# Lookup steps of 512 columns and whole grams in a DLRM interaction tower

## What is computed

```python
e = jnp.stack([tbl_0[ids[:, 0]], ..., tbl_25[ids[:, 25]]], axis=1)     # 2048 x 26 x 128
combined = jnp.concatenate([e, r_dense_x[:, None, :]], axis=1)
interact = jnp.einsum('bfd,bgd->bfg', combined, combined)
z = interact[:, _TRIU_I, _TRIU_J]                                      # 351 pairs
h = jnp.concatenate([z, r_dense_x], axis=1)
h = jnp.maximum(h @ W_top1 + b_top1, 0.0)                              # 479 -> 512
h = jnp.maximum(h @ W_top2 + b_top2, 0.0)                              # 512 -> 256
y = h @ W_top3                                                         # 256 -> 1
```

## Time and profile before

| | us |
|---|---|
| median of 3 executions | 373.93 (371.11 to 374.2) |
| the profiled execution | 374.13 |
| its span in the profile | 371.9 |
| TensorE busy | 345.5 |
| GpSimd busy | 258.8 |

### The profile page before, as it was taken

The page is one execution under the profiler, slowest core; times in us unless marked ns, Lnnn a source line. Parts: engine busy times, 40 slices in busy tenths (PEclk is TensorE's granted clock), DMA queues, the critical chain, the costliest instruction groups (busy, mean ns, idle before and its releaser), DMA issues.

```text
span 371.9 us, 13580 instructions
## 1 busy us (share of the span) xinstructions
PE 345.5 (93%) x6176; PEld 317.1 (85%) x6176; DVE 170.1 (46%) x380; ACT 184.4 (50%) x235; POOL 258.8 (70%) x265
## 2 busy tenths in 40 slices
PE   1998787989998999999999999999999999999997
PEld 0898776879897889999899998999899998899887
DVE  4589654533533435356245535356244635350220
ACT  3588242764345543473716643473725734376433
POOL 6688877777777777777777777777777777774000
PEclk9999899999998999999999999999999999999999
DMA  7967743211622126221262226321262222221000
GB/s 242 356 183 243 232 149 107 67 51 51 196 70 67 51 58 183 78 65 51 68 198 53 65 54 173 91 67 53 51 206 60 64 53 65 55 56 37 19 4 3
DMA packets 15917, 37.14 MB, mean 100 GB/s; under 512 B 5141, under 2 KB 7829, under 8 KB 15860
## 3 DMA queue, kind: packets, MB, share of 16 engines
q0 software_dynamic: 8192, 16.79, 16.9%
q1 hardware_dynamic: 7668, 19.48, 16.1%
HBM read 36.24 MB, written 0.01 MB: 97 GB/s over the span
## 4 chain that ended last, share of the span: by engine, by line
PE 69%; POOL 20%; issue 7%; DMA 3%; SPq 0%; ACT 0%
PE ps_lk L509 29%; POOL rows L242 20%; PE ps_gram L536 10%; PE ps_tr L521 6%; PE ps_zt L562 6%; PE ps_mlp L562 6%; PE ps_mlp L569 3%; PE ps_zt L569 3%; DMA zt<-in_tbl 2%; PE ps_mlp L577 1%; PE ps_lk L590 1%; PE ps_lk L489 1%; PE ps_zt L549 1%; DMA rows<-in_tbl,gather_ids 1%; PE ps_lk L597 0%
## 5 line engine op out<-in xcount | busy, mean ns | idle before, releaser
L242 POOL DMA_INDIRECT rows<-in_tbl,gather_ids x256 | 257.4, 1006 | 80.4 <-issue 76.2
L279 DVE TENSOR_SCALAR onehot<-ids_from 128x512 fp32r<-128x512 f32 x320 | 126.3, 446 | 94.1 <-PE ps_lk L509 68.7
L509 PE MATMUL ps_lk<-onehot,table 128*128 128x256 f32 x1248 | 163.3, 290 | 2.6 <-DVE onehot L279 2.0
L509 PEld LDWEIGHTS ps_lk<-onehot,table 128*128 128x128 f32 x1248 | 155.9, 196 | 4.3 <-issue 3.1
L360 ACT COPY xt<-ps_tr 128x512 f32<-128x512 f32 x64 | 77.0, 1203 | 93.0 <-PE ps_tr L521 91.2
L536 PEld LDWEIGHTS ps_gram<-xt 128*26 128x26 f32 x4096 | 44.1, 103 | 23.4 <-issue 20.7
L536 PE MATMUL ps_gram<-xt 128*26 128x26 f32 x4096 | 52.7, 192 | 9.8 <-issue 4.8
L350 ACT COPY xt<-ps_lk 128x512 f32<-128x512 f32 x40 | 48.9, 1236 | 14.5 <-PE ps_gram L536 10.5
L287 DVE STREAM_TRANSPOSE zs<-ps_gram 128x832 f32<-128x832 f32 x16 | 16.8, 1050 | 85.9 <-PE ps_gram L536 85.9
L521 PE MATMUL ps_tr<-ident,rows 128*128 128x128 f32 x256 | 39.3, 276 | 3.3 <-ACT xt L360 1.8
L521 PEld LDWEIGHTS ps_tr<-ident,rows 128*128 128x128 f32 x256 | 29.6, 140 | 7.1 <-ACT xt L360 2.4
(11 more groups left out here) (57 smaller groups left out, 153.7 us busy)
## 6 DMA issues: line engine op xcount, KB each, us to landing
ids<-in_ids_onehot SPq DMA_DIRECT2D x8, 768.0 KB
w<-in_tbl SPq DMA_DIRECT2D x8, 512.0 KB, 5.0
rows<-in_tbl,gather_ids POOLq DMA_INDIRECT x256
ids<-in_ids_onehot SPq DMA_DIRECT2D x7, 512.0 KB
dense_x<-in_dense SPq DMA_DIRECT2D x8, 128.0 KB
zt<-in_dense SPq DMA_DIRECT2D x8, 128.0 KB
ids<-in_ids_onehot SPq DMA_DIRECT2D x2, 256.0 KB, 4.1
h<-in_tbl SPq DMA_DIRECT2D x1, 512.0 KB, 5.9
```

The lines of the kernel that those rows point to most:

```text
L242: pool.indirect_dma_start(rows[n % ROW_BUFS][:, r, :], None, t_[f"tbl_{GATHERED[r]}"], bass.IndirectOffsetOnAxis(ap=gather_ids[:, n, r:r + ...
L279: nc.vector.tensor_scalar(onehot[:, u % RING, :, :], ids_from[:, 2 * i:2 * i + 2, :], float(k), None, ALU.is_equal).then_inc(s_unit, 1)
L509: m = nc.tensor.matmul(bank(c, i)[:, j, :], table[:, 2 * i + j, part, k, :], onehot[:, u % RING, j, :], start=(k == 0 and j == 0 and part ...
```

## The change

The samples of one step become four tiles (512 columns) and one table: 16 matmuls of 512 columns. The ten tables are split into two fives, `FIRST` and `SECOND`. Chunk 0 looks up the first five for tiles 0 to 3, and the second five for tiles 0 and 1 alone, two tables to a step as before; chunks 1 to 6 look up one of the fives in turn, for their own two tiles and the next two; the last chunk the second five for its own tiles. `xt` now holds four tiles, and only two row buffers are left. VectorE compares the loaded ids, still integers, with a column of row numbers; the shifts on ScalarE are gone. The ids come in a load of 256 KB for each step, in four buffers. Both halves of a gram stand back to back in TensorE's list (but for tiles 0, 1 and 14), and all sixteen gathers of tile n wait for the whole gram of tile n - 2. The order of the last chunk is another: tile 14 goes through its layers ahead of the last tile's gram.

```diff
-CS = CT * P
+XT = 2 * CT
+N = XT * P
+HALF = NO // 2
+FIRST, SECOND = list(range(HALF)), list(range(HALF, NO))
+BY_CHUNK = [tuple(SECOND[i:i + 2]) for i in range(0, HALF, 2)]
+for c in range(CHUNKS):
+    STEP0.append(len(STEPS))
+    if c == 0:
+        STEPS += [(c, XT, (i,)) for i in FIRST] + [(c, CT, b) for b in BY_CHUNK]
+    elif c == CHUNKS - 1:
+        STEPS += [(c, CT, b) for b in BY_CHUNK]
+    else:
+        STEPS += [(c, XT, (i,)) for i in (SECOND if c % 2 else FIRST)]
-ROW_BUFS = 3
+ROW_BUFS = 2
-LEAD = (0, 2, 8, 14, 20)
+LEAD = (0, 2, 6, 12, 20)
...
+            def load_ids(e):
+                if e >= IDS:
+                    sp.wait_ge(s_unit, (e - IDS + 1) * KT)
+                sp.dma_start(ids[e % IDS][:, :], t_["ids_onehot"][e:e + 1, :].to_broadcast([P, N])
...
                     elif b >= len(LEAD):
-                        pool.wait_ge(s_gpart, max(b - 2 * PARTS, 0) + 1)
+                        pool.wait_ge(s_gpart, (n - 1) * PARTS)
...
+            def make_units(e):
+                dve.wait_ge(s_ids[e % IDS], (e // IDS + 1) * 16)
+                for k in range(KT):
+                    if k % USE == 0 and e > 0:
+                        dve.wait_ge(s_unit_used, ((e - 1) * KT + k) // USE + 1)
+                    w = STEPS[e][1] * P * len(STEPS[e][2])
+                    nc.vector.tensor_scalar(onehot[:, k, 0:w], ids[e % IDS][:, 0:w], own[:, k:k + 1], None, ALU.is_equal
+                                            ).then_inc(s_unit, 1)
...
+            for c in range(1, CHUNKS - 1):
+                make_units(STEP0[c] + 4)
+                make_units(STEP0[c + 1])
+                make_units(STEP0[c + 1] + 1)
+                pack(c * CT)
+                make_units(STEP0[c + 1] + 2)
+                if c + 2 < CHUNKS:
+                    make_units(STEP0[c + 1] + 3)
+                pack(c * CT + 1)
...
+            def evac(e):
+                _, w, tables = STEPS[e]
+                a, f = NG + 1 + tables[0], len(tables)
+                act.wait_ge(s_unit_used, (e + 1) * KT // USE)
+                if w == XT:
+                    nc.scalar.copy(xt[:, :, a], ps_lk[e % LB][:, :]).then_inc(s_lk, 1)
...
+            def lookup(e):
+                c, w, tables = STEPS[e]
+                if e >= LB:
+                    pe.wait_ge(s_lk, e - LB + 1)
...
+                    for j, i in enumerate(tables):
+                        x = slice(j * w * P, (j + 1) * w * P)
                         for part in range(2):
+                            m = nc.tensor.matmul(ps_lk[e % LB][:, x], table[:, i, part, k, :], onehot[:, k, x],
...
             def gram(n, part):
                 if part == 0:
+                    pe.wait_ge(s_lk, STEP0[n // CT + 1])
...
+            for c in range(1, CHUNKS - 1):
+                a, e, f = c * CT, STEP0[c], STEP0[c + 1]
+                turn_pairs(a - 2)
+                if c == 1:
+                    turn(a, 0)
+                else:
+                    turn(a, 3)
+                    layer3(c - 2)
+                lookup(e + 3)
+                turn_pairs(a - 1)
+                if c == 1:
+                    turn(a, 1)
+                lookup(e + 4)
+                if c == 1:
+                    turn(a, 2)
...
+                layer1(c - 1, 0)
+                lookup(f)
+                if c == 1:
+                    turn(a, 3)
+                layer1(c - 1, 1)
+                gram(a, 0)
+                gram(a, 1)
+                turn(a + 1, 0)
+                layer1(c - 1, 2)
+                turn(a + 1, 1)
+                layer1(c - 1, 3)
+                turn(a + 1, 2)
+                lookup(f + 1)
+                turn(a + 1, 3)
+                layer2(c - 1, 0)
+                turn(a + 2, 0)
+                lookup(f + 2)
+                turn(a + 2, 1)
+                layer2(c - 1, 1)
+                turn(a + 2, 2)
+                gram(a + 1, 0)
+                gram(a + 1, 1)
+            c, a = CHUNKS - 1, TILES - 2
+            turn_pairs(a - 2)
+            turn(a, 3)
+            layer3(c - 2)
+            turn_pairs(a - 1)
+            layer1(c - 1, 0)
+            gram(a, 0)
+            turn(a + 1, 0)
+            layer1(c - 1, 1)
+            turn(a + 1, 1)
+            layer1(c - 1, 2)
+            gram(a, 1)
+            layer1(c - 1, 3)
+            turn(a + 1, 2)
+            layer2(c - 1, 0)
+            layer2(c - 1, 1)
+            turn_pairs(a)
+            layer3(c - 1)
+            last1(0, 0)
+            last1(0, 1)
+            turn(a + 1, 3)
+            last1(0, 2)
+            gram(a + 1, 0)
+            gram(a + 1, 1)
+            last1(0, 3)
+            turn_pairs(a + 1)
+            last2(0, 0)
+            last2(0, 1)
+            for j in range(T1):
+                last1(1, j)
+            for j in range(T2):
+                last2(1, j)
             last3()
```

More of the change, by code:

```diff
@@ L52 @@
 MLP_USES = T1 + T2 + 1
-LP = NO // 2
+assert PAIRS == NF * (NF - 1) // 2 and NO % 2 == 0
+RING = KT
+USE = 2
 LB = 3
[L58 to L63, removed]
+IDS = 4
 PARTS = 2
-LEAD = (0, 2, 8, 14, 20)
-SPLIT = list(range(2, NO)) + [0, 1]
+LEAD = (0, 2, 6, 12, 20)
+SPLIT = list(range(1, NO)) + [0]
 LAST = (CHUNKS - 1) * MLP_USES
@@ L121, in build @@
         s_gids = sem("s_gids")
[L122 to L125, removed]
+        s_ids = [sem(f"s_ids{b}") for b in range(IDS)]
         s_densex = sem("s_densex")
@@ L227, in _ @@
             load_dense_x(1)
+            for e in range(11, STEP0[2]):
+                load_ids(e)
             for c in range(1, CHUNKS):
                 if c + 1 < CHUNKS:
[L230 to L231 removed]
+                    for e in range(STEP0[c + 1], STEP0[c + 2]):
+                        load_ids(e)
                     load_dense_x(c + 1)
@@ L313, in _ @@
+            nc.vector.memset(ps_gram[:, :, :], 0.0).then_inc(s_zero, 1)
+            dve.wait_ge(s_const, 1)
+            nc.vector.tensor_copy(own[:, :], own_i[:, :]).then_inc(s_own, 1)
+            dve.wait_ge(s_own, 1)
+            dve.sem_inc(s_carrier["dve"], 1)
+            make_units(0)
+            for e in range(1, STEP0[1]):
+                for n in range(len(STEPS[e][2])):
+                    low(STEPS[e][2][n] - 1)
+                make_units(e)
             low(NO - 1)
             dve.wait_ge(s_const, 3)
-            make_units(1, 0, 2 * KT)
@@ L482, in lookup_first @@
             def lookup_first():
+                pe.wait_ge(s_raw[0], 16)
                 for k in range(KT):
                     pe.wait_ge(s_unit, k + 1)
-                    for j in range(2):
-                        if k == 0:
-                            pe.wait_ge(s_raw[j], 16)
-                        m = nc.tensor.matmul(bank(0, 0)[:, j, :], raw[j][:, k, :], onehot[:, k, j, :].bitcast(F32),
-                                             start=(k == 0 and j == 0), stop=(k == KT - 1), skip_group_check=True)
+                    m = nc.tensor.matmul(ps_lk[0][:, :], raw[0][:, k, :], onehot[:, k, :].bitcast(F32),
+                                         start=(k == 0), stop=(k == KT - 1))
@@ L507, in lookup @@
                         for part in range(2):
-                            m = nc.tensor.matmul(bank(c, i)[:, j, :], table[:, 2 * i + j, part, k, :],
-                                                 onehot[:, u % RING, j, :], start=(k == 0 and j == 0 and part == 0),
+                            m = nc.tensor.matmul(ps_lk[e % LB][:, x], table[:, i, part, k, :], onehot[:, k, x],
+                                                 start=(k == 0 and j == 0 and part == 0),
                                                  stop=(k == KT - 1 and part == 1), skip_group_check=True)
```

480 lines of the change are left out of this document (221 added, 259 removed).

## The result

| | before | changed |
|---|---|---|
| median, us (executions) | 374.06 (4) | 412.4 (4) |
| lowest to highest | 371.11 to 376.16 | 408.75 to 418.87 |
| profiled execution / its span | 374.13 / 371.9 | 413.38 / 411.6 |
| ratio, 95% interval | | 1.100 (1.088 to 1.112) |

The change costs 10%. The forecast was slower, 380.5, with a range up to 388: the direction was right, the size was far off. In a second job the changed kernel ran 411.45 beside 374.06, ratio 1.091 (1.084 to 1.098).

The account below looks back on a forecast made before the run. TensorE (93% busy) bounds the kernel, GpSimd closely second. Gram 3 ends at 114.9, five chunks of 43.6 reach 332.9, the end is 375.5; clock drops give 378.3, 2.2 outside the span 380.5. Own range 376 to 384; 8 in 10, 364 to 388.

Parts of the forecast that it names:

- the whole gram: Both gram halves back to back on TensorE: 256 instructions outrun their fetch, so 5.0 us each instead of 3.46.
- I take 3.46: A 512-column lookup step on TensorE takes 3.46 us for 3.92, saving 0.46 a step, 15.6 us over 34 steps.
- rival B: The lookup step stays at 3.92 us, a chunk becomes 45.1, time 388; chance 0.07.
- I charge two drops on the path at 1.4: TensorE's granted clock drops after gaps: two drops at 1.4 us each, moving the end from 375.5 to 378.3.
- Rival D: TensorE's clock drops more often, after every closing gram: six drops, 386 us; chance 0.14.
- A chunk becomes 43.6: Steady interval between layer-3 blocks grows to 43.6 us from 42.3, through fetch stops and gathers waiting for whole grams.
- the loop gather, turn, gram, release: Sixteen gathers wait for a whole gram, their rows for turns and the next gram; with 3.1 us of stops, takes TensorE's saving.
- the head: Start of the kernel: eight steps for five before the first gram, TensorE over 5 us in hand, no cost at the end.
- rival C: VectorE's integer compare takes 0.61 us instead of 0.39, making steps wait: 16 us in all, 396; chance 0.03.
- the tail: From the end of gram 13 at 332.9 to the kernel's end at 375.5, 42.6 us.

Follow-up runs that it names:

- Sixteens alone: The kernel before with all sixteen gathers of tile n waiting for the whole gram of tile n - 2, halves staying apart: 403.59 us, ratio 1.071.
- halves apart and eights: The changed kernel with other work between each gram's halves, gathers of half h waiting for half h of gram n - 2: 386.35 us, ratio 1.033.

## Why the prediction was wrong in its size

The forecast's 380.5 and the profiled 413.38 differ by 32.9. By the forecast's own stations: gram 3 was to end at 114.9 and ended at 123.1, 8.2 late; the five chunks to the end of gram 13 (361.6) were to take 218.0 and took 238.5, 20.5 more; from gram 13 to the end 42.6 were forecast and 50.0 taken, 7.4 more. Off that come the 2.8 that the forecast had added for the clock, and 0.4 of the time around the span.

**Right: the whole gram.** It was charged with 5.0; the 13 whole grams of the trace take 4.4 to 7.2 from their start to the next block's, 5.1 on average. The reason given, 256 instructions in less time than their fetch needs, is borne out: with whole grams the kernel before gets the same stops, with the halves apart the changed kernel loses them. The place of a stop is fixed by the count of instructions, too. In two traces of the changed kernel, from two jobs, the 14 stops lie behind the same matmuls (136 of 256 in gram 2, 167 in gram 3, and so on to 243 in gram 15), and in the kernel before with whole grams each stop lies 8 matmuls earlier in its gram than a chunk before (behind 202 in gram 4, then 194, 186, 178, 170, and 162 in gram 14). The fetch takes 3.45 us by the double stop, the forecast had 3.3. Beside the Trainium skill (page "Runtime: NRT & Kernel Launch", section "Instruction fetch mechanics"), which calls the cost of crossing a block limit mostly hidden, stand the 25.6 us of 15 stops in the kernel before with whole grams: the trace doesn't agree. Only the double stop (7.24 for one gram, where two fetch limits fall into it) was not foreseen.

**Wrong: "I take 3.46: the row streams just as many columns per weight load."** It measured 3.75, so a step saved 0.17 and not 0.46. The busy time of the lookups' group hardly moved: 163.1 us after, 163.3 before (in part at the lower clock). That was rival B, which "decides once a step is over 3.6". The step went 0.29 of the 0.46 between the two times, and by B's own sum that makes 380.5 + 7.5 x 0.29 / 0.46 = 385.2. It is 4.7 of the 32.9.

**Wrong: "I charge two drops on the path at 1.4."** There are ten slow groups, most of them behind a stop, and the one behind a closing gram costs 2.95 us: layer 3 0.75 more and the step 2.2 more. In the chunk shown both kinds appear. Against the forecast's own chain from the end of the closing gram (221.01): gram a ended after 21.6 for 20.8 (three steps at 3.75); TensorE reached the third turn after 40.2 for 37.4, since two more steps and a block and a turn at the lower clock lay before it, and the rows, forecast for 38.1, no longer mattered; the gram then took 7.24 for 5.0. The chunk is 47.9 for 43.6. Rival D (six drops, 386) named the mechanism and its price a drop was too small.

**Wrong: "A chunk becomes 43.6".** The forecast let the saving go "to the loop gather, turn, gram, release", as it did, and followed that loop for a TensorE at full speed, where GpSimd and TensorE meet within 0.1 us. It didn't ask what happens once either is late: nothing is left to take it up. In four of the five chunks the chain that ended last goes through the stop of gram a, then through the gathers that its end releases, and on to their rows and the next gram, as here (the chunk shown further up is the one without):

```profile
194.33 2.25 issue
196.58 1.09 PE ps_gram L570 x68
197.93 0.94 POOL rows L262
...
212.38 3.15 DMA rows<-in_tbl,gather_ids
```

So a late gram delays the gathers, and they the next gram; GpSimd's 34.6 us in 11 waits are the other side of it. Sixteens alone cost the kernel before 30.8 us by the medians (403.59 less 372.75), 27 by the ratio, which no line of the forecast held.

**Wrong: the head "costs nothing at the end".** It counted steps of TensorE and weighed the compares, 3.1 a step, but not the splits of the tables that VectorE makes among them. Each of the head's wide steps asks VectorE for eight compares and a split, 4.31 us from start to start, where TensorE needs 4.12 for the step and a turn. VectorE is full for 24 us and the gathers are held with it: gather 65, forecast for 92.2, starts at 100.13, and the gathers behind it don't make that up. The compare itself cost about what was said, 0.405 for 0.39, so rival C played no part.

**Wrong: the tail**, 42.6 by the forecast, lost 7.4. The stop of 2.03 in its gram isn't the cause: that gram took 4.5, less than the 5.0 charged. TensorE reached the last turn 27.0 us after the end of gram 13, for 22.5 in the forecast; in between a layer block waited 2.21 for the pairs' copy and then ran at the lower clock (3.78 for 1.9). From the last gram to the end it took 16.6 for 13.05, and 7 us of that at the lower clock. The forecast took both parts over from the kernel before, at full clock.

## What to carry to other kernels

Where two engines run within 2 or 3% of each other, don't price a change by its own stops alone: ask what takes up a delay of 2 us on either, and what the granted clock does behind it. Spread runs of very short instructions: in this kernel 256 of them in under 3.45 us stopped TensorE. And costs of this kind don't add: whole grams and sixteens each cost the kernel before some 30 us alone, and in the changed kernel undoing one brought 5 us or nothing and undoing both 25. So undoing one of two such edits says little; undo both.

## What the runs showed of the hardware

- A gather that meets a split of a table on VectorE isn't held for that instruction only. In the kernel with halves apart and eights the gather at 35.90 takes 5.93 us. It meets two splits and the whole run of eight compares behind them, and ends as that run ends (the changed kernel's trace of the same job has a gather of 5.93 too):

```profile
35.90 5.93 POOL L262 DMA_INDIRECT rows<-in_tbl,gather_ids  x1 [0.31 <-issue]
```

```profile
36.19 2.34 DVE L303 TENSOR_TENSOR table<-w,table 128x1024 fp32r<-128x1024 f32 x2
38.46 3.24 DVE L297 TENSOR_SCALAR onehot<-ids,own 128x512 fp32r<-128x512 int32 x8
```

  With the splits cut to 0.28 us the same compares leave gathers at 0.9 to 1.3. The Trainium skill (page "SBUF — State Buffer", section "SBUF: two separate sides") says that VectorE and GpSimd share a port pair as an exclusive lock, which the one that starts first gets for its whole instruction. That a gather is held agrees; 5.93 us is longer than any one instruction of VectorE there, the longest of which takes 1.2.

- In four of the seven jobs the kernel before took 32 to 35% longer, other kernels up to 51%, and TensorE crawled inside grams. The kernel before with whole grams, in such a job:

```profile
200.53 0.28 PE L536 MATMUL ps_gram<-xt 128*26 128x26 f32 x6 [0.48 <-issue]
201.29 0.27 PE L536 MATMUL ps_gram<-xt 128*26 128x26 f32 x6 [0.49 <-issue]
202.06 0.26 PE L536 MATMUL ps_gram<-xt 128*26 128x26 f32 x5 [0.50 <-issue]
203.50 0.25 PE L536 MATMUL ps_gram<-xt 128*26 128x26 f32 x4 [1.19 <-issue]
```

  One to six matmuls come at a time, every 0.7 or 1.4 us, with nothing awaited. In the kernel before, whole grams cost 21 to 23% there instead of 9%. It looks like the same shortage of instructions, drawn out, but that is a guess: its cause wasn't tried.
